# Second products of two feed-forward stages with tokens as the stationary operand, summed by token in PSUM

## The reference, cut to what matters

```python
x = x + jnp.tanh(g_xattn[0]) * _L0_xattn_ref(ctx_1024, _layernorm(x), ...)
x = x + jnp.tanh(g_ffn[0]) * _L0_ffn_ref(_layernorm(x), ...)
x = x + jnp.tanh(g_xattn[1]) * _L1_xattn_ref(_layernorm(x), ctx_1024, ctx_1024, ...)
x = x + jnp.tanh(g_ffn[1]) * _L1_ffn_ref(_layernorm(x), ...)

# _L0_ffn_ref: 8 zones, the best 3 of each batch row by a router
for e in range(N_ZONES):
    z = jax.nn.gelu(x @ Wa[e]) @ Wb[e]          # 256 -> 1024 -> 256
    zone_outputs = zone_outputs + z * w[:, e, None, None]
return x + zone_outputs

# _L1_ffn_ref: integer weights over 127
h = jax.nn.silu(x @ wg.T) * (x @ wu.T)          # 256 -> 768
return h @ wd.T                                  # 768 -> 256
```

## Time and profile before

| what | us |
|---|---|
| median of 3 runs | 681.62 |
| lowest and highest of them | 681.37, 685.14 |
| the profiled execution, its own time | 680.97 |
| its span | 679.2 |
| PE busy | 614.7 |
| DVE, ACT, POOL busy | 385.6, 369.5, 147.5 |
| mean granted clock of PE | 0.98 |

### The profile page before, as it was taken

The page is one execution under the profiler, slowest core; times in us unless marked ns, Lnnn a source line. Parts: engine busy times, 40 slices in busy tenths (PEclk is TensorE's granted clock), DMA queues, the critical chain, the costliest instruction groups (busy, mean ns, idle before and its releaser), DMA issues.

```text
span 679.2 us, 10341 instructions
## 1 busy us (share of the span) xinstructions
PE 614.7 (91%) x3676; PEld 470.5 (69%) x3676; DVE 385.6 (57%) x841; ACT 369.5 (54%) x630; POOL 147.5 (22%) x218
## 2 busy tenths in 40 slices
PE   2699888888799999999999999999778998999997
PEld 2475555554478888888888787787556776868885
DVE  6677667779573524425556435433586564556653
ACT  4316748566785746556657435545776344353432
POOL 9633265254640000000000000001564210210000
PEclk9879999999899999999999999999999999999999
DMA  7320120122030030300302340020132100000000
GB/s 232 98 83 15 33 55 13 48 50 97 19 124 15 0 124 0 106 20 0 125 22 73 83 137 1 7 88 2 44 98 73 25 2 2 2 32 1 32 31 32
DMA packets 22546, 34.68 MB, mean 51 GB/s; under 512 B 4704, under 2 KB 13280, under 8 KB 22496
## 3 DMA queue, kind: packets, MB, share of 16 engines
q1 hardware_dynamic: 20224, 30.51, 14.4%
q0 software_dynamic: 1984, 3.44, 2.1%
q10 hardware_dynamic: 288, 0.07, 0.0%
HBM read 18.93 MB, written 2.10 MB: 31 GB/s over the span
## 4 chain that ended last, share of the span: by engine, by line
PE 74%; DVE 11%; ACT 6%; POOL 5%; issue 4%; DMA 0%; ACTq 0%; DVEq 0%; POOLq 0%
PE SC L1254 29%; PE PV L1254 24%; PE AUX L1254 6%; PE PV L1273 4%; PE AUX L1359 3%; PE SC L1389 3%; DVE NM L1135 2%; DVE O L1143 2%; ACT XN L845 2%; ACT PB L898 1%; PE AUX L1316 1%; DVE ST L1057 1%; PE PV L1359 1%; POOL QG L739 1%; DVE XL L999 1%
## 5 line engine op out<-in xcount | busy, mean ns | idle before, releaser
L999 DVE TENSOR_TENSOR HL<-HF,HH 128x512 fp32r<-128x512 f32 x96 | 67.4, 702 | 153.8 <-ACT HH L940 153.7
L898 ACT ACTIVATE PB<-SC 77x1024 f32<-77x1024 f32 x96 | 95.1, 1014 | 61.2 <-PE SC L1389 61.1
L940 ACT ACTIVATE HH<-PV 128x512 fp32r<-128x512 f32 x96 | 57.4, 598 | 66.6 <-PE SC L1254 66.6
L935 ACT ACTIVATE HF<-PV 128x512 f32<-128x512 f32 x96 | 57.4, 598 | 54.5 <-PE PV L1254 52.8
L710 POOL TENSOR_TENSOR RSTD<-RSTD,NHALF 128x4 f32<-128x4 f32 x16 | 17.8, 1113 | 292.6 <-DVE RSTD L1070 292.5
L1254 PE MATMUL PV<-XH,WAH 128*128 128x512 f32 x192 | 77.6, 404 | 1.0 <-DVE O L1143 1.0
L1254 PE MATMUL SC<-HH,WBH 128*128 128x512 f32 x192 | 76.3, 397 | 0.0
L1254 PE MATMUL SC<-HH,WBL 128*128 128x512 f32 x192 | 75.8, 395 | 0.0
L1254 PE MATMUL PV<-XH,WAL 128*128 128x512 f32 x192 | 75.3, 392 | 0.0
L1254 PE MATMUL PV<-XL,WAH 128*128 128x512 f32 x192 | 75.3, 392 | 0.0
L1254 PE MATMUL SC<-HL,WBH 128*128 128x512 f32 x192 | 74.9, 390 | 0.0
(11 more groups left out here) (256 smaller groups left out, 1200.6 us busy)
## 6 DMA issues: line engine op xcount, KB each, us to landing
QG<-QH SPq DMA_DIRECT2D x96, 64.0 KB, 2.0
WSA<-in_wa SPq DMA_DIRECT2D x6, 1024.0 KB, 5.0
WSB<-in_wb SPq DMA_DIRECT2D x12, 512.0 KB, 6.8
QG<-QL SPq DMA_DIRECT2D x48, 64.0 KB, 2.0
X<-in_x SPq DMA_DIRECT2D x4, 512.0 KB, 6.1
QG<-QH POOLq DMA_DIRECT2D x32, 64.0 KB, 2.2
out_x<-X SPq DMA_DIRECT2D x8, 256.0 KB, 2.0
QG<-QL POOLq DMA_DIRECT2D x16, 64.0 KB, 2.3
```

Of the source, the lines that this page charges most:

```text
L898: act.activation(probs(n)[0:S, :, :], scores(n)[0:S, :, :], ACT.Exp, scale=SCALE[a]).then_inc(exp_done, 1)
L935: act.activation(HF[s % 2][:, :], PV[:, s % 2, :], ACT.Gelu_apprx_tanh)
L940: act.activation(HH[s % 2][:, :], PV[:, s % 2, :], ACT.Gelu_apprx_tanh).then_inc(act_done, 1)
L999: return dve.tensor_tensor(dst, raw, hi.bitcast(F32), ALU.subtract)
```

## The change

The second products of both feed-forward stages are turned round. A new helper `token_sums` takes a block of 128 tokens of `HH`/`HL` (or `GH`/`GL`) as the stationary operand and all 256 output features of the weights as the moving one, so each second product of a step is 12 matmuls of 256 columns where it was 6 of 512. The sums stand by token in the same PSUM banks: bank i holds the token blocks 2i and 2i + 1. The steps `evac` and `out` are gone from the plan, with their entries in `PARTS` and `LOAD`, the tile `YS`, and the auxiliary banks they took; a step `sum` stands where `evac` stood, and in it DVE adds each PSUM bank to `X` (FFN0: one `tensor_tensor` a bank; FFN1: one `scalar_tensor_tensor` a bank with the scale `TG[:, 4:5]`). `ys_ready` now counts half tiles, by DVE. SP sends a half tile out when its sum is there. ACT waits for nothing of `out` at its first exp of the second attention.

```diff
-PARTS = {"turn": (3, KC), "query": (3, KC), "turn_mix": (2, KC), "project": (2, 2), "out": (3, 2)}
-LOAD = {"attend": 2, "values": 3, "max": 1, "negmax": 2, "turn": 2, "turn_mix": 2, "project": 3, "out": 2}
+PARTS = {"turn": (3, KC), "query": (3, KC), "turn_mix": (2, KC), "project": (2, 2)}
+LOAD = {"attend": 2, "values": 3, "max": 1, "negmax": 2, "turn": 2, "turn_mix": 2, "project": 3}
...
             if (s - LAG) % HC == HC - 1:
-                atoms[-1] += [("evac", FFN1, (s - LAG) // HC)]
+                atoms[-1] += [("sum", FFN1, (s - LAG) // HC)]
...
-        side.setdefault(end + LAG, []).append(("evac", FFN0, j))
-        side.setdefault(end + LAG + 1, []).append(("out", FFN0, j))
+        side.setdefault(end + LAG, []).append(("sum", FFN0, j))
...
-    steps += [("zone_end",), ("evac", FFN0, 3), ("query", 1, 2), ("out", FFN0, 3)]
+    steps += [("zone_end",), ("sum", FFN0, 3), ("query", 1, 2)]
...
-    at(side, 5, ("out", FFN1, 0, 0))
-    at(side, 6, ("out", FFN1, 0, 1))
...
-    at(side, 7, ("out", FFN1, 1, 0))
-    at(side, 8, ("scale", FFN1, 3), ("out", FFN1, 1, 1))
+    at(side, 8, ("scale", FFN1, 3))
...
-    at(side, 25, ("out", FFN1, 2, 0))
-    at(side, 26, ("out", FFN1, 2, 1))
...
-              ("evac", FFN1, 3), ("out", FFN1, 3)]
+              ("sum", FFN1, 3)]
...
-        YS = place("YS", [P, KC, NT], F32)
...
@@ SP @@
-                elif kind == "out" and step[1] == FFN1:
-                    _, _, j, i = step
-                    used(sp, step)
-                    sp.dma_start(out[j][:, 2 * i:2 * i + 2, :],
-                                 X[:, TT * j + 2 * i:TT * j + 2 * i + 2, :]).then_inc(stored, 16)
+                elif kind == "sum" and step[1] == FFN1:
+                    j = step[2]
+                    for i in range(2):
+                        sp.wait_ge(ys_ready, 2 * (J + j) + i + 1)
+                        sp.dma_start(out[j][:, 2 * i:2 * i + 2, :],
+                                     X[:, TT * j + 2 * i:TT * j + 2 * i + 2, :]).then_inc(stored, 16)
...
@@ ACT @@
-                    if n == A0_UNITS:
-                        filled(act, ("out", FFN0, J - 1, 1))
...
-                elif kind == "evac":
-                    _, stage, j = step
-                    n = order[step]
-                    if n:
-                        filled(act, OUTS[n - 1])
-                    if stage == FFN0:
-                        act.wait_ge(y_done, zone_end_of(j))
-                    for c in range(KC):
-                        if stage == FFN1:
-                            act.wait_ge(gy_done if c else gy_half, HC * (j + 1) if c else j + 1)
-                        if stage == FFN0:
-                            ins = act.activation(YS[:, c, :], SC[:, j % 2, c, :], copy)
-                        else:
-                            ins = act.activation(YS[:, c, :], SUMS[c], copy, scale=TG[:, 4:5])
-                    ins.then_inc(ys_ready, 1)
...
@@ DVE @@
+                            if stage == ATT1:
+                                dve.wait_ge(ys_ready, 2 * (j + 1))
                             for i in range(2):
-                                used(dve, ("out", FFN0, j, i) if stage == ATT1 else ("project", j, i))
+                                if stage == FFN1:
+                                    used(dve, ("project", j, i))
...
-                elif kind == "out":
-                    _, stage, j, i = step
-                    filled(dve, step)
-                    xi = X[:, TT * j + 2 * i:TT * j + 2 * i + 2, :]
-                    if stage == FFN0:
-                        dve.wait_ge(added, j + 1)
-                    dve.tensor_tensor(xi, bank(step).rearrange("p (t d) -> p t d", t=2), xi, ALU.add).then_inc(frees(step), 1)
+                elif kind == "sum":
+                    _, stage, j = step
+                    for i in range(2):
+                        xi = X[:, TT * j + 2 * i:TT * j + 2 * i + 2, :]
+                        if stage == FFN0:
+                            dve.wait_ge(added, j + 1)
+                            dve.wait_ge(y_done, zone_end_of(j))
+                            dve.tensor_tensor(xi, SC[:, j % 2, i, :].rearrange("p (t d) -> p t d", t=2), xi,
+                                              ALU.add).then_inc(ys_ready, 1)
+                        else:
+                            dve.wait_ge(gy_done if i else gy_half, HC * (j + 1) if i else j + 1)
+                            dve.scalar_tensor_tensor(xi, SUMS[i].rearrange("p (t d) -> p t d", t=2), TG[:, 4:5], xi,
+                                                     ALU.mult, ALU.add).then_inc(ys_ready, 1)
...
@@ PE @@
+            def token_sums(ps, i, hi, lo, wh, wl, first, last):
+
+                for t in (2 * i, 2 * i + 1):
+                    block = slice(P * t, P * (t + 1))
+                    for n, (lhs, rhs) in enumerate(((hi, wh), (hi, wl), (lo, wh))):
+                        ins = pe.matmul(ps[:, D * (t % 2):D * (t % 2 + 1)], lhs[:, block], rhs,
+                                        start=first and t == 2 * i and n == 0, stop=last and t == 2 * i + 1 and n == 2)
+                return ins
+
             def zone_out(s):
...
                 if first and z:
-                    pe.wait_ge(ys_ready, nt + 1)
-                for c in range(KC):
-                    cols = slice(P * c, P * (c + 1))
-                    ins = product(SC[:, nt, c, :], [(WBH[:, f, cols], WBL[:, f, cols], HH[s % 2][:, :], HL[s % 2][:, :])],
-                                  start=first, stop=last)
+                    pe.wait_ge(ys_ready, 2 * (nt + 1))
+                for i in range(2):
+                    ins = token_sums(SC[:, nt, i, :], i, HH[s % 2], HL[s % 2], WBH[:, f, :], WBL[:, f, :], first, last)
...
             def gated_out(s):
...
-                        pe.wait_ge(ys_ready, J + j)
+                        pe.wait_ge(ys_ready, 2 * (J + j))
...
+                for i in range(2):
+                    ins = token_sums(SUMS[i], i, GH[s % 2], GL[s % 2], WNH[:, f, :], WNL[:, f, :], f == 0, f == HC - 1)
+                    if i == 0 and f == HC - 1:
                         ins.then_inc(gy_half, 1)
...
                     if a == 1 and n < A0_UNITS + 2:
-                        pe.wait_ge(ys_ready, 3 + n - A0_UNITS)
+                        pe.wait_ge(ys_ready, 2 * (3 + n - A0_UNITS))
...
-                elif kind == "out":
-                    _, stage, j, i = step
-                    pe.wait_ge(ys_ready, order["evac", stage, j] + 1)
-                    ps = fill(step)
-                    for t in (2 * i, 2 * i + 1):
-                        for c in range(KC):
-                            at_c = D * (t % 2) + P * c
-                            ins = pe.transpose(ps[:, at_c:at_c + P], YS[:, c, P * t:P * (t + 1)], ident[:, :])
-                    ins.then_inc(aux_ready, 1)
```

More of the change, by code:

```diff
@@ L579, in flamingo @@
         NORMS = [s for s in PLAN if s[0] == "norm"]
-        OUTS = [s for s in PLAN if s[0] == "out" and s[3] == 1]
         MIXED_UNITS = unit(1, 2, 0)
```

5 lines of the change are left out of this document (removed).

## The result

The kernel after takes 678.53 us, the median of 7 runs (677.61 to 679.59), beside 683.14 for the kernel before in the same series (680.84 to 685.14). The ratio is 0.9941, with a 95% interval of 0.9923 to 0.9959: 4.0 us less (2.8 to 5.3), where 12.6 less were forecast. The sign held, the size did not, and 669.0 with its range up to 674.0 is missed.

What follows compares the result with a forecast made beforehand. PE was taken to bound the zone stage and last gated steps, a chain of small waits the second attention. Terms -1.5 - 4.0 - 1.6 - 2.6 - 1.2 + 0.3 - 2.0 = -12.6 us gave 669.0 us, range 665.5 to 674.0.

Steps and rivals of the forecast that it cites:

- Part 1: Second products, 120 steps: 12 matmuls of 256 columns at the projection's price, 1.378 us against 1.39; -1.5 us, ends -3.0 and +2.4.
- The rival of the dearer matmul: Second products: 121 ns a matmul because ACT and DVE work on SBUF; 12 cost 1.452, sum -3.7, 677.9 us; chance 0.10.
- Part 2: Zone stage: transposes for tiles 0 to 2 and PE's 1.23 us wait for DVE's add go; -4.0 us.
- Part 3: Passage to the second attention, tile 3: first exp 2.1 us earlier, first statistics 1.6 earlier; -1.6 us, ends 0 and -2.1.
- Part 4: Gated stage: six halves of four transposes, tiles 0 to 2, at 0.44 us each go; -2.6 us.
- The wait of 1.20: Blended list, tile 3: attention units 4 and 5 come apart, ending PE's wait for an exp; -1.2 us, ends 0 and -1.2.
- Part 5: Gated stage: DVE's sum ahead of GF waits for the second product and delays tile 0's up product; +0.3 us, ends 0 and +4.2.
- Step 8: Gated stage: sign of being right, PE idle less than 0.3 us before this step's up product.
- Steps 13 and 19: Gated stage: sign of being wrong, PE idle there with GF or the sum as releaser.
- Part 6: Kernel end: last add can start where ACT's last copy did, 0.07 us longer than that copy; -2.0 us.

Runs made afterwards that it cites:

- columns sweep: Changed kernel plus groups of 24 matmuls on PE alone behind its end, moving width 128 to 512 and fewer stationary columns; 119.6 ns at 256, 227.1 at 512.
- probe: Changed kernel plus groups of 36 matmuls of 256 columns on PE alone behind its end; 718.7 us with the added work.
- old products: Changed kernel with second products put back to 6 matmuls of 512 columns, for timing only; 672.41 us, ratio to before 0.9857.
- later norm: Changed kernel with the gated stage's tile 2 last statistics and norm one attention unit later; 679.53 us, ratio to before 0.9952.
- new products: Kernel before with only its second products exchanged for 12 matmuls of 256 columns, for timing only; 690.42 us, ratio 1.0110.
- hybrid: The later norm's kernel with zone-stage tiles 0 and 1 back to 6 matmuls of 512 columns, evac and out; 679.07 us, ratio to before 0.9950.
- shifted before: Kernel before with everything from PB on, feed-forward weights included, 64 bytes further up in SBUF; 677.66 us, ratio to before 0.9921.
- halves: Changed kernel with matmuls ordered pass by pass, so the written half of the PSUM bank changes with every matmul; 677.58 us in one run.
- shift: Changed kernel with everything from PB on (HH, HL, GH, GL and feed-forward weights) 64 bytes further up in SBUF; 677.59 us, ratio to before 0.9920.
- apart: Changed kernel with HH, HL, GH, GL alone moved 64 bytes, weights kept modulo 128; 677.01 us, ratio to before 0.9925.
- crossed: Changed kernel with all feed-forward weights moved 64 bytes, HH and GH kept; 673.40 us, ratio to before 0.9865.
- four runs of PE alone: Kernels with extra matmul groups on PE alone behind the end: probe, columns sweep, offsets, and the change's 512/256 pattern on the apart kernel (12 in 1.409 to 1.447 us).
- offsets: Changed kernel plus groups of 24 matmuls on PE alone, blocks cut at varied element offsets; GH 119.2 ns at offset 0, 117.5 at 16.

## Why the prediction was right or wrong

**Part 1 failed, and with it the sum.** The step reads "I stay at the projection's price, since it is the same instruction form on the same data types, between the same neighbours": 1.378 us for 12, -1.5 us. They take 1.436, and the products cost 5.8 to 7.5 us. Two things were missing. Narrow matmuls are dearer by the column: 2 of 256 cost 239 ns where one of 512 costs 227 to 231, and by the columns sweep that isn't only the load, since a load of 32 columns left 117.8. And "the same" left out the tiles: `XH` stands 64 bytes apart from `WOH`, `HH` and `GH` alike with their weights. Apart, 12 take 1.41; that is the dearer of the three readings from the earlier trace rows, and it gave +2.4 us as an end of the term. So the tiles account for some 0.025 of the 0.058 us by which 1.378 was missed. The rest, and how the projection gets down to 1.365, stay open: PE alone gave 117.8 ns for the same instructions on the same tiles.

The rival of the dearer matmul came close, with 1.452 and a sum of -3.7, but for a reason that fell in the probe; that closeness is luck.

**Part 2 held.** Forecast -4.0; the zone stage with old products is 4.1 shorter. PE's wait of 1.23 us for the add is gone, and nothing took its place.

**Part 3 held in its link, less in its size.** First exp and scaling of the layer norm on ACT, first statistics on DVE (the last query copy starts at 484.46):

```profile
485.05 1.92 ACT L889 ACTIVATE PB<-SC 77x1024 f32<-77x1024 f32 x2
...
489.97 2.07 ACT L838 ACTIVATE XN<-X,RSTD 128x256 f32<-128x256 f32 x4 [1.36 <-POOL RSTD L706]
```

```profile
485.85 1.39 DVE L1036 BATCH_NORM_STATS2 ST<-X 128x6 f32<-128x256 f32 x4
```

From the last query copy to the exp it is 0.59 us now, 2.80 before: -2.2 (forecast -2.1). To the statistics 1.39, before 3.08: -1.7 (forecast -1.6). But the scaling starts 489.97 - 484.46 = 5.51 us behind the copy, before 488.27 - 481.63 = 6.64 in the same view: only -1.1, as POOL's power behind the statistics took 1.58 us where it took 1.01. That is no chance: it took 1.58 in every kernel with the step `sum` and 1.01 in the three with `out` behind the zone stage. Why isn't shown. The passage as a whole is 2.4 shorter; the rest of that is the clock, below.

**Part 4 held, and was paid back.** Gate product to gate product over tile 1's transposes took 631.33 - 626.39 = 4.94 us before and 632.09 - 627.90 = 4.19 after: 0.75, and 0.8 a tile without the product's 0.05; -2.4 for three, with tile 0, where more moves at once, taken like this one. The wait of 1.20 is gone, as the attention of unit 5 stands behind the up product, at 598.12, without a wait. Yet the stall of 1.08 us in step 10 is new and takes it back, and it comes from the same new order (part 5).

**Part 5 failed in its place.** Step 8 came as forecast: `GF` ends at 588.98 behind the two scaled adds, and the up product starts at 589.15 with no wait. Steps 13 and 19 had none either. The stall came elsewhere: the up product of step 10 waits for the `GF` of step 9, and that is late. The tile's last statistics stand ahead of this `GF` on DVE, but they stood there before the change too, with one more add of 0.6 us. What is new is DVE's wait for PE, before the change and after it:

```profile
599.27 0.71 DVE L1143 STREAM_TRANSPOSE O<-PV 128x512 f32<-128x512 f32 x1
...
602.21 0.67 DVE L1221 SCALAR_TENSOR_TENSOR GF<-SG,SC 128x512 f32<-128x512 f32 x1
```

```profile
601.32 0.72 DVE L1122 STREAM_TRANSPOSE O<-PV 128x512 f32<-128x512 f32 x1 [1.52 <-PE PV L1258]
...
603.67 0.67 DVE L1206 SCALAR_TENSOR_TENSOR GF<-SG,SC 128x512 f32<-128x512 f32 x1
```

The attention's product with the values (`PV<-PB,V`) started at 597.76, ahead of the second product, and starts at 600.17 now, behind it: one more thing that the mixing by `LOAD` moved when `out` left the list. The prediction popped the list by hand and said that it "changes in one place that matters"; this is a second one, and only DVE's wait shows it. So +1.1 instead of +0.3. Moving the statistics away (the later norm) did free this `GF`, and let another instruction be late.

**Part 6 held.** The last add:

```profile
674.18 0.28 PE L1267 MATMUL AUX<-WNH,GL 128*128 128x256 f32 x1
674.50 0.75 DVE L1180 SCALAR_TENSOR_TENSOR X<-AUX,TG,X 128x512 f32<-128x512 f32 x1
```

It ends 1.07 us after the last matmul's start, 3.15 before; the end of the kernel is 2.0 shorter (forecast -2.0).

**The clock moved, and not by the change.** In the profile of before it fell behind an idle stretch at 524. After has none there and one at 573, to 0.50, the lower of the two levels (1.2 of 2.4 GHz) (stretch, length, PE busy, PEld, DVE, ACT, POOL, clock):

```profile
570.00:573.00 3.00, 1.39 (x7) 1.04 (x8) 1.29 (x2) 0.60 (x1) 0.00 (x0) 0.92 0.00 0
573.00:576.00 3.00, 3.00 (x10) 2.06 (x9) 0.00 (x0) 0.31 (x1) 0.00 (x0) 0.51 0.00 0
```

The kernel before has the same idle time there, and no fall:

```profile
570.00:573.00 3.00, 1.46 (x7) 1.24 (x8) 1.29 (x2) 0.55 (x1) 0.00 (x0) 1.00 0.00 0
573.00:576.00 3.00, 3.00 (x17) 2.36 (x16) 0.02 (x1) 2.29 (x4) 0.00 (x0) 1.00 0.00 0
```

The stretch from the seventh to the eighth gate product holds it: 6.70 us before, 8.34 after, and 8.30 to 8.36 with old products, new products, later norm, hybrid and the shifted before, but 6.75 to 6.78 in halves, shift, apart, crossed and the four runs of PE alone: 6 of 15 profiled executions have it. It comes and goes with both forms, as does the one of 0.50 in the new products' passage, costs 1.6 us here, and hides the gain of part 4 in the table's column (135.54 twice): 24 products at +0.05 are +1.2, the transposes -2.4, the wait of 1.20 against the stall of 1.08 some -0.1, the fall +1.6, together +0.3 where the column says 0.0.

**The sum again**, for parts 2 to 6 without the clock: -4.1 - 1.1 - 2.4 - 1.2 + 1.1 - 2.0 = -9.7, and old products against before measured -9.8. In the passage the clock gave back some 1.2 of the 2.4: from the layer norm's scaling to the first gate product it is 42.55 us before and 41.35 after, but 42.41 to 42.49 in probe, columns and offsets, the same kernel there with falls of the clock in that stretch. So the two effects of the clock nearly cancel in these profiles, which is chance. Add the products' 5.8 and it is the -4.0 of after.

## What to carry to other kernels

Where PE is full, a product with the same columns in narrower matmuls is not free: price the pair of load and matmul at the width in question, with the operands' own tiles, before exchanging 6 x 512 for 12 x 256; here halving the width cost 0.05 us in 1.39 and ate more than half of what standing sums by token saved. Before that, try where the operands stand: 64 bytes in SBUF were worth more than the change, 5.4 us in the kernel before for one line, 5 in the one after. Measure such a placement in the whole kernel, as prices of single pairs don't add up: of three placements of the kernel after, one gained. And when a step leaves a mixed list, follow what moves on every engine and who waits for it, not the exchanged instruction alone.

## What the runs showed of the hardware that I had not expected

A matmul with its own 128-column load costs some 110 to 112 ns from 128 to 224 moving columns, 119.6 at 256 and 227.1 at 512, with no other engine at work. With 256 moving columns, a load of 64 columns gives 113.6 and one of 32 again 117.8.

Its price depends on where the stationary and the moving block stand to each other modulo 128 bytes: 256 columns 117.5 ns apart and 119.2 to 119.7 alike. With 512 columns the layout matters as well, but no price for the pair comes out: alike 226.7 where only such matmuls run and 231 in the shift, apart 228 or 233 for the same pair in one trace. What ran just before changes the price (in apart, the 512-column group went from 1.384 to 1.400 with its own tiles unchanged). The Trainium skill, "TensorE: Matmul & The Clock Gate", section "Step-by-step: what each phase is for", has two independent read ports for the two operands, so that loading takes nothing from the running matmul. Taken by itself, that leaves no room for an effect of their distance; here there is one, and the measurement decides. What happens between them isn't shown by these runs.

The granted clock fell to 0.50 between the same two gate products in 6 of 15 profiled executions and not in the other 9, with nearly the same idle time beside it (1.39 us busy of 3 in after, which fell, and 1.46 in before, which did not), so a difference of 1.6 us in one stage between two single profiles proves nothing by itself.
